# A new order of the pieces in a decoder layer whose attention and key/value work share TensorE

## What is computed

```python
x = x + self_attention(layernorm(x))          # 16 heads of 32, causal, q and k rotated
x = x + cross_attention(layernorm(x), ctx)    # 16 heads of 32, 722 keys, no mask
x = x + experts(layernorm(x))                 # 8 experts, softmax gates, the best 2
```

## Time and profile before

| | us |
|---|---|
| median of 3 runs (lowest, highest) | 1438.62 (1435.73, 1440.55) |
| the profiled execution's own time | 1441.02 |
| its span in the trace | 1439.2 |
| iteration -1 and the start | to about 101 |
| one of iterations 0 to 14 | about 62.7 at first, about 63.2 from 450 us on |
| iteration 15 | about 1041 to 1111 |
| experts | to the end, PE busy 245.75 of the last 249.00 |

### The profile page before, as it was taken

How to read it: one execution, slowest core, us unless ns; L and a number is a source line. 1 busy time by engine, 2 the same in 40 slices (tenths; PEclk the granted TensorE clock), 3 DMA queues, 4 the chain that set the end, 5 groups by cost and what they waited for, 6 DMA issues and landing times.

```text
span 1439.2 us, 43985 instructions
## 1 busy us (share of the span) xinstructions
PE 1341.8 (93%) x19700; PEld 856.9 (60%) x19700; DVE 901.2 (63%) x1463; ACT 614.7 (43%) x888; POOL 684.5 (48%) x642
## 2 busy tenths in 40 slices
PE   4689999999999999999999999999956799999999
PEld 4365766667576666757676675767644444444444
DVE  4657777686777768677776867777563443333332
ACT  4236555555655555564555556455534010000000
POOL 1435757666575666657576665757555100000000
PEclk9899999999999999999999999999967699999999
DMA  7011010101101010110101011010201100101002
GB/s 269 1 39 32 9 44 3 45 8 40 38 8 45 2 45 8 39 38 8 45 3 44 8 40 37 10 45 3 82 31 37 54 30 4 35 36 36 8 0 92
DMA packets 27538, 50.37 MB, mean 35 GB/s; under 512 B 1612, under 2 KB 13188, under 8 KB 27356
## 3 DMA queue, kind: packets, MB, share of 16 engines
q1 hardware_dynamic: 27356, 47.62, 10.2%
HBM read 41.06 MB, written 6.55 MB: 33 GB/s over the span
## 4 chain that ended last, share of the span: by engine, by line
PE 85%; DVE 7%; POOL 3%; ACT 2%; issue 1%; DMA 1%; SPq 0%; POOLq 0%; ACTq 0%; DVEq 0%
PE psum L254 58%; PE psum L664 7%; PE psum L753 6%; PE psum L738 4%; DVE c_most L986 2%; PE psum L682 2%; PE psum L641 2%; DVE c_max L991 2%; PE psum L633 1%; DMA arena<-in_L_attn_Wv 1%; PE psum L345 1%; PE psum L366 1%; POOL arena L1157 1%; PE psum L597 1%; PE psum L649 1%
## 5 line engine op out<-in xcount | busy, mean ns | idle before, releaser
L1157 POOL TENSOR_TENSOR arena<-prob,arena 128x1200 f16<-128x1200 f32 x128 | 314.3, 2467 | 188.3 <-ACT arena L847 188.3
L986 DVE TENSOR_REDUCE c_most<-psum 100x4 f32<-100x1444 f32 x128 | 211.5, 1652 | 21.0 <-PE psum L738 18.8
L254 PE MATMUL psum<-w_kv,cT 128*128 128x512 f16 (+1 forms) x864 | 199.7, 379 | 0.5
L254 PE MATMUL psum<-cT,w_kv 128*128 128x361 f16 x1152 | 196.4, 322 | 0.0
L477 DVE SCALAR_TENSOR_TENSOR w_self_all<-psum,g_now,w_self_all 128x512 f32<-128x512 f32 x104 | 77.8, 750 | 168.6 <-PE psum L254 168.6
L838 ACT ACTIVATE prob<-psum 128x1200 f32<-128x1200 f32 x128 | 149.8, 1170 | 70.5 <-PE psum L753 56.6
L847 ACT ACTIVATE arena<-prob 128x1200 f16<-128x1200 f32 x128 | 151.3, 1196 | 1.5
L254 PEld LDWEIGHTS psum<-cT,w_kv 128*128 128x128 f16 x1152 | 106.0, 99 | 65.2 <-issue 4.0
L254 PEld LDWEIGHTS psum<-w_kv,cT 128*128 128x128 f16 (+1 forms) x864 | 83.4, 101 | 90.6 <-DVE c_raw L901 5.1
L954 DVE SCALAR_TENSOR_TENSOR arena<-psum,b_part,arena 128x361 f16<-128x361 f32 x128 | 74.3, 591 | 86.1 <-ACT arena L819 86.1
L829 ACT ACTIVATE cv<-psum 128x512 f16<-128x512 f32 x96 | 57.3, 597 | 163.0 <-PE psum L254 163.0
(11 more groups left out here) (179 smaller groups left out, 2175.6 us busy)
## 6 DMA issues: line engine op xcount, KB each, us to landing
c_raw<-in_ctx SPq DMA_DIRECT2D x16, 960.0 KB
cT<-in_L_ffn_expert_w SPq DMA_DIRECT2D x4, 1024.0 KB, 5.2
cv<-in_L_ffn_expert_w SPq DMA_DIRECT2D x4, 1024.0 KB, 5.3
x_in<-in_x SPq DMA_DIRECT2D x16, 200.0 KB
x_scratch<-x_out SPq DMA_DIRECT2D x16, 200.0 KB
w_self_all<-x_scratch SPq DMA_DIRECT2D x12, 256.0 KB, 4.4
out<-w_self_all SPq DMA_DIRECT2D x12, 256.0 KB, 2.0
c_raw<-in_ctx SPq DMA_DIRECT2D x16, 123.0 KB
```

The source lines that it names most:

```text
L254: last = pe.matmul(out_ap, a(pa), b(pb), start=(i == 0 and j == 0), stop=(i == len(pairs) - 1 and j == 2))
L986: dve.tensor_reduce(c_most[:, hf], score[0:L, :, 0:HC], AXIS.X, ALU.max).then_inc(max_done, 1)
L1157: pool.tensor_tensor(prob16[o % 2][:, (2 + part) * PT:(3 + part) * PT], prob[:, part], prob16[o % 2][:, part * PT:(part + 1) * PT], ALU.su ...
```

## The change

Only the table differs. The names in it are the same 116.

```diff
 STEPS = [
-    ["low3a", "X1T", "low3b", "max_A0", "CX0", "A0", "SQ"],
-    ["B0", "max_B0", "CX1", "rotate_q", "SK"],
-    ["MX0", "CX2", "CX3", "rotate_k", "CX4"],
-    ["T0a", "exp0a", "CX5", "PV3"],
-    ["T0b", "SS0", "SS1", "exp0b", "shift0", "scale_heads", "max_A1", "CK0"],
-    ["A1", "CK1", "shift1", "CK2"],
-    ["B1", "high0a", "max_B1", "TT", "low0a", "self_exp0", "SV"],
-    ["MX1", "bias_x", "high0b", "self_sum0", "CV0"],
-    ["T1a", "low0b", "SS2", "SS3", "exp1a", "CK3"],
-    ["T1b", "shift2", "PV0", "exp1b", "self_scale0", "shift3"],
-    ["A2", "max_A2", "self_scale1", "self_exp1", "self_sum1", "SP0", "CV1"],
-    ["B2", "SP1", "self_scale2", "high1a", "self_scale3", "max_B2", "TP", "high1b", "low1a", "SP2", "SP3",
-     "CV2", "low1b"],
-    ["MX2", "CV3"],
-    ["T2a", "exp2a", "SO", "CK4"],
-    ["T2b", "exp2b", "CK5", "high2a", "low2a", "max_A3", "CK6"],
-    ["A3", "OP", "high2b"],
-    ["B3", "stats_mid", "max_B3", "CV4", "norm_mid", "CV5", "bias_mid"],
-    ["MX3", "X2T", "low2b", "PV1"],
-    ["T3a", "exp3a", "stats_x", "CQ", "norm_x", "high3a"],
+    ["low3a", "X1T", "CX0", "A0", "low3b", "max_A0", "CX1", "SQ"],
+    ["B0", "max_B0", "SK", "rotate_q"],
+    ["MX0", "CX2", "CX3", "CX4", "rotate_k", "exp0a", "CX5"],
+    ["T0a", "PV3"],
+    ["T0b", "high0a", "SS0", "SS1", "scale_heads", "exp0b", "shift0", "shift1", "bias_x", "self_exp0",
+     "max_A1", "SV"],
+    ["A1", "low0a", "max_B1", "CV0"],
+    ["B1", "high0b", "CV1", "low0b", "TT", "CK0"],
+    ["MX1", "self_sum0", "CV2", "SS2", "SS3", "self_scale0"],
+    ["T1a", "exp1a", "CK1", "shift2", "SP0"],
+    ["T1b", "shift3", "exp1b", "self_scale1", "self_exp1", "high1a", "self_sum1", "TP", "self_scale2",
+     "max_A2", "SP1"],
+    ["A2", "CK2", "self_scale3", "low1a", "CK3", "high1b", "max_B2", "SP2"],
+    ["B2", "PV0", "low1b", "SP3", "CV3"],
+    ["MX2", "CV4", "SO"],
+    ["T2a", "exp2a", "exp2b", "CK4"],
+    ["T2b", "max_A3", "CK5"],
+    ["A3", "OP", "high2a", "high2b", "low2a"],
+    ["B3", "stats_mid", "max_B3", "CK6", "norm_mid", "CV5", "low2b"],
+    ["MX3", "X2T", "bias_mid", "exp3a", "stats_x", "PV1"],
+    ["T3a", "CQ", "high3a", "norm_x"],
     ["T3b", "exp3b", "CK7", "split_cq", "PV2", "high3b"],
 ]
```

## The result

The changed kernel takes **1490.94 us** (median of 6 runs, 1489.02 to 1494.91) against 1438.94 (6 runs, 1434.79 to 1440.55) for the kernel before: ratio 1.0372, interval 1.0350 to 1.0394. It is 3.7% slower. The forecast had the sign, and neither the size (+8 forecast, +52 measured) nor the range. The profiled execution has a span of 1493.1 us.

A forecast was written before the change was run, and what follows sets the result against it. PE was taken as the bound, busy 61.60 of 62.70 us per full iteration. Full iterations +12, iteration 15 -4, iteration -1 0: +8, so 1446.6 us; range 1434.6 to 1458 by the bounds, 1424 to 1456 for 8 in 10.

The forecast's parts named there:

- group 3: Join before MX3: held some 0.5 us by norm_mid's last instruction as before, MX3 0.3 sooner; +0.1 us per iteration.
- Start of an iteration: A0 to MX0: CX1 fills SQ's 0.36 us gap, and a wait of 0.35 appears before MX0; sum 0.
- Group 1: low0b holds the join; banks queued behind it delay MX1 by 0.7 and CV2 by 0.5 us; +0.5 per iteration.
- Group 2: low1b holds the join; MX2 waits 0.1 us and CV4 0.3, where no gap was before; +0.4 per iteration.
- A full iteration: Each of the 15 full iterations: +0.8 us taken (bounds 0.4 to 1.2), together +12.
- Iteration 15: Last iteration, without prep: shorter waits of exp1b and exp2a, less 2 us for a held join; -4 us, bounds 0 and -8.5.
- Iteration -1: Before the first A0: SP1 waits instead of SP0, about as long; 0 us, bounds -1.5 and +1.5.
- The joins run free: Rival: joins of groups 1 and 2 start before POOL's low parts and are not held; 1424.6 us, chance 0.26.
- Pairing pays: Rival: PE drains less often, 1.4 us per piece saved over 15 iterations, inside "within 0.3%"; chance 0.02.

The follow-up runs named there:

- with the pause: The changed kernel, its order kept, with POOL waiting for x_norm's signal ahead of low2b in iterations 0 to 14: 1446.44 us, ratio 1.0065.

## Why the prediction was wrong

**The step that failed** is group 3: "norm_mid's last instruction holds the join some 0.5, as it did ... +0.1." It kept the instruction that holds the join and did not look at what comes behind it. In the new table low2b took bias_mid's place. Measured: a join of 3.01 us, a gap of 2.39 before MX3, and in 10 of 15 iterations 1.5 us more of slowed matmuls behind it. That is 45.6 us over the 15 iterations (1004.2 in the changed kernel, 958.6 with the pause). In the five iterations that ran at full clock the difference between the two is 2.1 to 2.5 us, so the gap makes some 34 of it and the lowered clock the other 12 or so (two iterations of the kernel with the pause had a lower clock too).

The two rules that I set against the trace did not contain it. I wrote that a join that starts while a long POOL instruction runs ends when that instruction ends; in the new table it does so in groups 0, 1 and 2. The Trainium skill, SBUF — State Buffer, section SBUF: two separate sides, has the shared ports as a lock held for a whole instruction by whichever starts first, for a VectorE instruction with two SBUF inputs. The trace agrees as far as that goes (1.94 and 1.42 us in groups 1 and 2, 0.17 with one operand in all 64). By either rule I ended the wait with the instruction that was running; in group 3 it went on through the next one, and that was worth 45.6 us.

**Start of an iteration:** right. The gap before SQ is gone, 0.17 before MX0 (forecast 0.35).

**Group 1:** right. With c at 251.77, where B1 starts on PE, low0b starts at c+1.87 and the join at c+2.42 (forecast 1.9 and 2.4). The join takes 1.94 (forecast about 1.9), MX1 waits 0.57 for CV0's low part and not for c_max (forecast 0.7), CV2 waits 0.29 (forecast 0.5). Taking CV0's low part out of that queue gave 0.56 us per iteration.

**Group 2:** right. The join takes 1.42 as forecast; MX2 starts with no gap (forecast 0.1), and from MX2 to CV4 it is 0.3 longer than from MX0 to CX2.

**A full iteration without group 3's miss:** forecast +12 over the 15, measured +11.0 (958.6 with the pause against 947.6). That kernel's 1446.44 us stand beside the forecast of 1446.6. The single waits come out too if PE is read from start to start, iteration 6 of the kernel with the pause against iteration 6 of the new table with one-operand joins (63.36 against 61.39 us). The pieces ahead of MX0, MX1, CV2 and MX3 are longer by 0.32, 0.73, 0.51 and 0.12, and those around MX2 by 0.47; the forecast had 0.35, 0.7, 0.5, 0.1 and 0.4. That the whole time agrees is partly luck, since the next term was off too.

**Iteration 15:** the sign right, the size not: -7.3 for -4. The timeline of ACT in the changed kernel:

```profile
1135.66 1.17 ACT L839 ACTIVATE prob<-psum 128x1200 f32<-128x1200 f32 x1 [0.90 <-POOL arena L1158]
...
1147.52 1.17 ACT L839 ACTIVATE prob<-psum 128x1200 f32<-128x1200 f32 x1 [1.11 <-POOL arena L1158]
...
1152.09 1.17 ACT L839 ACTIVATE prob<-psum 128x1200 f32<-128x1200 f32 x1 [3.40 <-POOL arena L1158]
```

exp1b's wait fell from 5.03 to 0.90, exp2a's from 3.47 to 1.11, and a new one of 3.40 before exp2b gives part back, so ACT's waits alone don't add up to 7.3. Of the 7.3 us between A0 and A3, 5.5 is less idle time of PE (17.6 us for 23.1) and 1.8 less busy time, at a granted clock of 0.76 for 0.71. The 2 us that I took off for a held join of group 1 were wrong: it took 0.17 us.

**Iteration -1:** +6.0 in the profiled execution where 0 was forecast, with bounds of 1.5. At full clock the new order costs about 1 us there (95.8 to 97.1 against 94.8 to 95.9), inside the bounds. The other 5 came with the lower clock, which six of ten executions with the new order show and none of four with the old; the forecast had no term for it. It had SP1 wait about as long as SP0 had (1.66 us), and SP1 waits 2.92.

**The rivals.** *The joins run free* did not happen: both of groups 1 and 2 were held. Its price can't be set against a run as it stands: with all joins at 0.17, those of groups 0 and 3 too, the new table takes 1412 to 1414 us, where it had 1424.6 for groups 1 and 2 alone. *Pairing pays* is out as a cause here, since both tables have 16 stretches; and a stretch more costs 0.20, so the 0.09 of one end is about half of it. What came true was none of the three: group 3's join, held by POOL's next instruction, which I had priced at +0.1 with no bound on it. By the rows a bound was there to be had: if the next low part also holds the join, it costs 2.46 less what DVE has in hand.

## What to carry to other kernels

When pieces change places on GpSimd, follow each short VectorE instruction with two SBUF operands through what is running as it arrives and also through what comes right behind that; a pause of 0.08 us between the two decided 45 us here. Better, take the short instruction out of the contest: one operand from SBUF in place of two made every join 0.17 us. That gave 1.2% with the old table and 1.7 to 1.9% with the new one, where the best order alone gave 0.2%. And price a reordering with such a side effect removed before judging its idea: the two tables are nearly equal in the full iterations once the joins are free, and the new one is ahead by iteration 15.

## What the runs showed that I had not expected

- A VectorE instruction of 100x8 elements with two SBUF operands took anything from 0.17 to 3.02 us, by what ran on GpSimd and what followed it there. With one operand it took 0.17 throughout.
- The clock behind the same gap of about 2.4 us fell in 10 of 15 iterations and stayed full in 5 (windows at 224.20 and 291.50: mean granted clock 0.74 and 1.00, so part of the first at 1.2 GHz and all of the second at 2.4). With a gap of 1.82 us it fell in 2 of 15. Why it falls in the one and not in the next was not settled.
- With the join arriving in bias_mid PE's gap before MX3 was 3.72 us and an iteration took 68.7 to 70.6 us (the first 66.9), though the join itself was shorter (2.69). CK6 ahead of max_B3, that one change of order, took the time from 1449.73 to 1523.87 (one execution).
